# Gated two-layer stack on one core: vector pieces of one link each, layer-1 scores over 32 rows, and the last two transposed blocks of the feed-forward in one operation

## What is computed

```python
x = x + tanh(g_x[0]) * xattn0(layernorm(x), ctx, mask)   # "A": 4 heads of 64, one K/V head, rotary
x = x + tanh(g_f[0]) * ffn0(layernorm(x))                # "F": width 704, inputs in blocks of 16 on an FP4 grid
x = x + tanh(g_x[1]) * xattn1(layernorm(x), ctx)         # "B": 16 heads of 16, biases, no mask
x = x + tanh(g_f[1]) * moe(layernorm(x))                 # "R" routes (top 2 of 8 experts), "M" computes, width 1024
```

```python
Q = (query @ Wq + bq).reshape(B, Tq, 16, 16).transpose(0, 2, 1, 3)
K = (key @ Wk + bk).reshape(B, Tk, 16, 16).transpose(0, 2, 1, 3)
scores = einsum('bhtd,bhsd->bhts', Q, K) / sqrt(16)
ctx = einsum('bhts,bhsd->bhtd', softmax(scores), V)
```

## Time and profile before

| | |
|---|---|
| median of 3 runs | 1644.17 us (1643.66 to 1647.43) |
| profiled execution, its own time | 1642.42 us |
| its span, first to last instruction | 1640.8 us |
| busy over the span: PE, DVE, ACT, POOL | 1400.4, 1117.3, 993.4, 413.3 us |
| mean granted clock of PE | 0.949 |

### The profile page before, as it was taken

How to read it: one execution, slowest core, us unless ns; L and a number is a source line. 1 busy time by engine, 2 the same in 40 slices (tenths; PEclk the granted TensorE clock), 3 DMA queues, 4 the chain that set the end, 5 groups by cost and what they waited for, 6 DMA issues and landing times.

```text
span 1640.8 us, 35711 instructions
## 1 busy us (share of the span) xinstructions
PE 1400.4 (85%) x11645; PEld 1072.6 (65%) x11646; DVE 1117.3 (68%) x2887; ACT 993.4 (61%) x2861; POOL 413.3 (25%) x560
## 2 busy tenths in 40 slices
PE   2567789989999889989998671999999999999994
PEld 1445556665666566656664430888888888888883
DVE  7977779899988999899986534344444454444452
ACT  1244778888888888888876760444445444455542
POOL 0101011211122211212111112334433444344442
PEclk9587999999999999999999975999999999999997
DMA  6020132112320223203220005551231412322214
GB/s 192 13 87 30 62 103 103 45 61 104 103 92 21 95 104 103 72 33 104 94 94 8 8 14 179 177 162 32 33 112 30 114 32 35 108 35 32 35 31 123
DMA packets 63158, 123.58 MB, mean 75 GB/s; under 512 B 13955, under 2 KB 51967, under 8 KB 58879
## 3 DMA queue, kind: packets, MB, share of 16 engines
q1 hardware_dynamic: 45743, 102.75, 18.0%
q0 software_dynamic: 17312, 19.56, 7.2%
HBM read 78.64 MB, written 48.04 MB: 77 GB/s over the span
## 4 chain that ended last, share of the span: by engine, by line
PE 52%; DVE 32%; ACT 8%; issue 5%; DMA 2%; POOL 1%; SPq 0%; DVEq 0%; ACTq 0%; POOLq 0%
PE bank L1401 15%; PE bank L1403 14%; PE bank L1402 14%; DVE b_mn L1121 4%; ACT b_ex L746 3%; PE bank L1483 2%; PE bank L1495 2%; DVE wm L1238 1%; DVE f_hs L1182 1%; DVE split_room L1265 1%; DVE wm L1190 1%; PE bank L1719 1%; DVE x L1176 1%; DVE wm L1196 1%; DVE wm L1201 1%
## 5 line engine op out<-in xcount | busy, mean ns | idle before, releaser
L1401 PE MATMUL bank<-split_room,wm 128*128 128x256 f16 x1152 | 314.9, 273 | 8.2 <-issue 6.8
L1378 DVE SCALAR_TENSOR_TENSOR split_room<-bank,b12e,split_room 128x256 f32<-128x256 f32 x288 | 138.2, 484 | 265.6 <-ACT split_room L900 260.8
L1402 PE MATMUL bank<-split_room,wm 128*128 128x256 f16 x1152 | 314.8, 273 | 0.0
L1403 PE MATMUL bank<-split_room,wm 128*128 128x256 f16 x1152 | 314.7, 273 | 0.0
L900 ACT ACTIVATE split_room<-bank,b12e 128x256 f32<-128x256 f32 x288 | 134.2, 470 | 196.0 <-PE bank L1403 194.2
L746 ACT ACTIVATE b_ex<-bank,b_mn 128x120 f32<-128x120 f32 x512 | 177.0, 361 | 36.9 <-DVE b_mn L1121 28.0
L1403 PE MATMUL bank<-wm,split_room 128*128 128x256 f16 x576 | 157.0, 273 | 0.0
L1401 PE MATMUL bank<-wm,split_room 128*128 128x256 f16 x576 | 157.0, 273 | 0.0
L1402 PE MATMUL bank<-wm,split_room 128*128 128x256 f16 x576 | 157.0, 273 | 0.0
L692 POOL DMA_INDIRECT acc<-split_room,m_cur x72 | 116.1, 1612 | 133.0 <-ACT split_room L914 106.1
L1483 PE MATMUL bank<-b_k,b_q 128*128 128x480 f32 x256 | 131.8, 597 | 14.6 <-ACT b_q L834 14.6
(11 more groups left out here) (356 smaller groups left out, 3616.3 us busy)
## 6 DMA issues: line engine op xcount, KB each, us to landing
split_room<-in_L_ffn_W SPq DMA_DIRECT2D x48, 512.0 KB, 8.0
wsplit<-split_room SPq DMA_DIRECT2D x16, 1536.0 KB, 6.6
wm<-wsplit SPq DMA_DIRECT2D x16, 1536.0 KB, 8.5
acc<-x SPq DMA_DIRECT2D x17, 256.0 KB, 2.2
xin<-in_x SPq DMA_DIRECT2D x16, 256.0 KB
rows<-r_row SPq DMA_DIRECT2D x16, 256.0 KB, 3.7
ct<-in_ctx SPq DMA_DIRECT2D x16, 120.0 KB
cb<-in_ctx SPq DMA_DIRECT2D x16, 120.0 KB, 2.6
```

Of the source, the lines that this page charges most:

```text
L1378: dve.scalar_tensor_tensor(m_h[:, c % 3], bank[c % 4][:, TILE:2 * TILE], b12e[:, p, 1, c:c + 1], m_s[:, c % 2], ALU.add, ALU.mult).then_in ...
L1401: pe.matmul(o, lh, rh, start=start, stop=False)
L1402: pe.matmul(o, ll, rh, start=False, stop=False)
L1403: return pe.matmul(o, lh, rl, start=False, stop=stop)
```

## The change

- Every chain on DVE is cut so that a stage holds one link; the new pieces are named `A.ln_1`, `F.q0a_1`, `R.logit_3` and so on. The operations stay the same.
- B's scores: b_k is now [128, 2, 2, 120]; a group of 32 rows holds two heads, and each of the two copies keeps one of them, so a matmul of 32 rows and 240 columns gives two heads and two of them a round. Head columns of wq1, wk1 and the biases are permuted (`head_order`), b_k is written by two operations over all partitions, and `pair` issues the scores of rounds k and k+1 as four matmuls over 32 rows each, alternating between two row groups and the two banks. The pair waits for the exponentials of all earlier rounds, and DVE's minimum of either round waits for the pair.
- `f_ht_`: blocks 4 and 5 are taken out by one operation on ACT and one on DVE.
- bq arrives by 8 small transfers in place of one, wq1, wk1 and bk are split in portions, and b_k is no longer cleared.
- FIRST, ORDER and LAST are new on all engines. In a steady step DVE's list goes from 57 to 95 entries and PE's from 54 to 50.

The core of the diff:

```diff
-        b_k = sb("b_k", [P, NK, 2, QUAD, S])
+        b_k = sb("b_k", [P, NK, 2, S])
...
-                for j in range(QUAD):
-                    h = slice(PITCH * j, PITCH * (j + 1))
-                    for a in range(2):
-                        last = act.activation(b_k[h, :, a, j], bank[2][h, 0:NK * S].rearrange("p (c s) -> p c s", c=NK), ACT.Copy, scale=C[h, C_M + a:C_M + a + 1])
+                for f in range(2):
+                    last = act.activation(b_k[:, :, f], bank[2][:, 0:NK * S].rearrange("p (c s) -> p c s", c=NK), ACT.Copy, scale=C[:, C_M + f:C_M + f + 1])
...
+                def pair(b, k0):
+                    if k0 == 0:
+                        pe.wait_ge(B.q, b + 1)
+                        pe.wait_ge(B.k, b + 1)
+                    else:
+                        pe.wait_ge(B.exp, b * n + k0)
+                    for e in range(NK):
+                        for k in (k0, k0 + 1):
+                            t, r = k // per, k % per
+                            h = slice(PITCH * r, PITCH * (r + 1))
+                            last = pe.matmul(sbks[k % 2][:, e * 2 * S:(e + 1) * 2 * S], q[h, e, t * P:(t + 1) * P], kk[h, e], start=True, stop=True)
+                            if e == NK - 1:
+                                last.then_inc(B.s_mm, 1)
...
-                        dve.wait_ge(G.s_mm, b * n + k + 1)
+                        dve.wait_ge(G.s_mm, b * n + (k + 1 if G is A else k // 2 * 2 + 2))
...
-                    act.activation(f_ht[:, 0, 4, c], bank[7][:, 0:P], ACT.Copy)
-                    act.activation(f_ht[0:FF0 - 5 * P, 0, 5, c], bank[7][0:FF0 - 5 * P, P:2 * P], ACT.Copy).then_inc(F.hq_hi, 1)
+                    act.activation(f_ht[:, 0, 4:6, c], bank[7][:, 0:2 * P].rearrange("p (c q) -> p c q", c=2), ACT.Copy).then_inc(F.hq_hi, 1)
...
-                    dve.tensor_tensor(f_ht[:, 1, 4, c], bank[7][:, 0:P], f_ht[:, 0, 4, c], ALU.subtract)
-                    dve.tensor_tensor(f_ht[0:r_, 1, 5, c], bank[7][0:r_, P:2 * P], f_ht[0:r_, 0, 5, c], ALU.subtract).then_inc(F.hq_lo, 1)
+                    dve.tensor_tensor(f_ht[:, 1, 4:6, c], bank[7][:, 0:2 * P].rearrange("p (c q) -> p c q", c=2), f_ht[:, 0, 4:6, c],
+                                      ALU.subtract).then_inc(F.hq_lo, 1)
...
+            def f_scale(n):
+                v, m, sc = F_PARTS[n]
+
+                def stage(b, p):
+                    cf.go_on(b)
+                    cf.wait()
+                    cf.link(dve.tensor_scalar(sc[:, 0], sc[:, 2], SIXTH, 1e-12, ALU.mult, ALU.max))
+                return stage
...
+                        for c in range(2):
+                            for a in range(2):
+                                for k in range(NK):
+                                    k_ = slice(k, k + 1)
+                                    split(head_order(st1[:, n_ - 1, k_], c, a, True)[:, 0],
+                                          head_order(w[:, 0, k_], c, a, False)[:, 0], head_order(w[:, 1, k_], c, a, False)[:, 0])
```

More of the change, by code:

```diff
@@ L369, in gated_stack @@
         FIRST = {
[L370 to L371 removed]
[7 rows of a table removed]
[L379 removed]
[11 rows of a table removed]
[L391 removed]
[8 rows of a table removed]
[L400 removed]
+            "SP": ("W@0 A.load@2 B.load@0 B.load@1 A.load@3 W@1 W@2 A.load@4 W@3 B.load@2 B.out@0 B.load@3 R.rank@0").split(),
@@ L444, in gated_stack @@
+            "POOL": ("R.ln@13 R.scatter@13 B.ln@15 R.ln@14 R.scatter@14 R.ln@15 R.scatter@15").split(),
[6 rows of a table added]
+                "B.t6@15 B.t7@15 B.rx1@15 B.r7@15 B.o1@15 R.z@15 R.t@15 R.logit@15").split(),
[11 rows of a table added]
+                "R.rank_4@15 R.rank_5@15 R.rank@15").split(),
[6 rows of a table added]
+                "B.p4@15 B.t5@15 B.t6@15 B.p5@15 B.t7@15 B.p6@15 B.p7@15 B.out@15 R.t@15 R.logit@15 R.rank@15").split(),
         }
@@ L1130, in stage, with values @@
                         ca.link(dve.reciprocal(rd[:, t], pv[:, :, width]))
+                    return stage
+                def values(k):
+                    def stage(b, p):
+                        t = k // per
+                        pv = pbks[t][:, 0:heads * (width + 1)].rearrange("p (h d) -> p h d", h=heads)
+                        ca.go_on(b)
                         ca.wait()
@@ L1137, in rounds @@
                 if G is A:
-                    made.update({f"{G.name}.p{k}": values(k) for k in range(per - 1, n, per)})
+                    made.update({f"{G.name}.p{k}": shares(k) for k in range(per - 1, n, per)})
+                    made.update({f"{G.name}.p{k}_1": values(k) for k in range(per - 1, n, per)})
                 return made
@@ L1205, in f_p @@
-            def f_p(b, p):
-                dequantise(f_z[:, :, :].rearrange("p t d -> p (t d)"), f_m, f_qs[:, 0], b, 0)
-            def f_pt(t):
-                def stage(b, p):
-                    dequantise(f_h[:, t], f_hm[:, t], f_hs[:, t, 0], b, 1 + t)
-                return stage
-            def f_q_in(b, p):
-                cf.go_on(b)
-                dve.wait_ge(F.z, b + 1)
-                for part in (quantise_a, quantise_b):
-                    part(f_z[:, :, :].rearrange("p t d -> p (t d)"), f_m, f_qs, b, 0)
@@ new lines, in f_scale, with stage, f_inverse @@
+            def f_scale(n):
+                v, m, sc = F_PARTS[n]
+                def stage(b, p):
+                    cf.go_on(b)
+                    cf.wait()
+                    cf.link(dve.tensor_scalar(sc[:, 0], sc[:, 2], SIXTH, 1e-12, ALU.mult, ALU.max))
+                return stage
+            def f_inverse(n):
+                v, m, sc = F_PARTS[n]
+                def stage(b, p):
+                    cf.go_on(b)
+                    cf.wait()
+                    dve.reciprocal(sc[:, 1], sc[:, 0]).then_inc(F.v, 1)
+                return stage
@@ new lines, in f_scaled, with stage, f_grid @@
+            def f_scaled(n):
+                v, m, sc = F_PARTS[n]
+                def stage(b, p):
+                    dve.wait_ge(F.v, b * 3 + n + 1)
+                    dve.tensor_tensor(blocks(v), blocks(v), over(sc[:, 1], BLK), ALU.mult).then_inc(F.u, 1)
+                return stage
+            def f_grid(n):
+                v, m, sc = F_PARTS[n]
+                def stage(b, p):
+                    dve.wait_ge(F.abs, b * 3 + n + 1)
+                    dve.tensor_scalar(m, m, 1.5, STEP, ALU.max, ALU.mult).then_inc(F.m, 1)
+                return stage
@@ new lines, in f_round, with stage, f_unshift @@
+            def f_round(n):
+                v, m, sc = F_PARTS[n]
+                def stage(b, p):
+                    dve.wait_ge(F.m, b * 3 + n + 1)
+                    dve.scalar_tensor_tensor(v, v, BELOW, m, ALU.mult, ALU.add).then_inc(F.t, 1)
+                return stage
+            def f_unshift(n):
+                v, m, sc = F_PARTS[n]
+                def stage(b, p):
+                    cf.go_on(b)
+                    dve.wait_ge(F.t, b * 3 + n + 1)
+                    cf.link(dve.tensor_tensor(v, v, m, ALU.subtract))
+                return stage
@@ L1228, in f_q, with f_unscale, stage @@
+            def f_unscale(n):
+                v, m, sc = F_PARTS[n]
+                def stage(b, p):
+                    cf.go_on(b)
+                    cf.wait()
+                    dve.tensor_tensor(blocks(v), blocks(v), over(sc[:, 0], BLK), ALU.mult).then_inc(F.hq, 1)
                 return stage
```

191 lines of the change are left out of this document (112 added, 79 removed), and 129 rows, old and new, of tables (FIRST, LAST, ORDER).

## The result

The changed kernel takes 1674.89 us (median, 1674.34 to 1679.25) against 1644.01 us before: a ratio of 1.019 with an interval of 1.017 to 1.021, so 1.9% slower. The forecast was 1610 us, faster. The profiled execution has a span of 1673.8 us against 1640.8 us.

What follows compares the result with a forecast made beforehand. No engine is full in the 52.2 us step; waits and small gaps on DVE, with PE close, bound it. Twelve steps at 49.2 us give -36 us, lead-in 0, tail +2: span 1606.8, median 1610 us, range 1580 to 1640.

Steps and rivals of the forecast that it cites:

- Part 1: DVE chains cut into pieces: 22 boundaries with other work between, 0.12 us each, 2.6 us less a step (bounds 0 to 5.0).
- One sign: DVE's busy time a step should stay near 47 us, its share rising to about 95%.
- Part 2: Scores over 32 rows on PE: a pair of rounds takes 1.2 us instead of 1.8, 2.4 us of PE less a step.
- Part 3: b_k copies on ACT, two operations instead of eight: 0.7 us instead of 3.21, 2.5 us less a step.
- part 4: f_ht blocks joined: one DVE operation of 0.42 us, saving 0.06 us a call, 0.1 us a step; ACT gains as little.
- part 5: Wait for both rounds: ring 4.9 us, +1.0 us a pair where exposed; in steady steps DVE's work between pairs covers it.
- the sum for the steady step: 52.2 us less 2.6 (pieces), 0.1 (f_ht) and 0.3 (long waits): 49.2 us a step, twelve steps -36 us.
- Part 6: Lead-in before the steady steps taken as 0 (-8 to +8 us); moved loads and POOL entries cost nothing; tail +2 us.
- rival (b): Slower: the wait for both rounds exposes 1.35 us at all four pairs, step 54.6 us, 1679 us in all; chance 0.08.
- The prediction's last sign: The prediction is wrong if the new list brings DVE waits over 3 us a step resting on no old row.
- the size of the end: Tail with two batches of exposed pairs: 7 x 1.0 us more, less 2 x 2.5 us of b_k: +2 us (-4 to +9).
- The start: Lead-in before the steady steps: some 5 us more DVE work against savings in the first batches, taken as 0 (-8 to +8).

Runs made afterwards that it cites:

- a_late2_fill: Changed kernel with R.scatter issued in the next step behind A.t's copies, plus 6 unread matmuls ahead of B.t0 on TensorE: 1623.3 us, 0.989 of the kernel before.
- a_fill: Changed kernel plus 28 unread matmuls a step on TensorE, 12 ahead of B.t0 and 16 behind F.gu0: 1645.4 us, 1.003 of the kernel before.
- b_pairwait: Kernel before with old matmuls and order, scores of both rounds issued together behind all earlier exponentials (TensorE's half of the join only): 1720.3 us, ratio 1.048.
- a_late2_exp: Changed kernel with R.scatter in the next step behind A.t's copies, plus a one-element exponential ahead of R.z on ScalarE: 1641.3 us, 0.999 of the kernel before.
- a_late: Changed kernel with R.scatter's four transfers issued in the next step, behind R.ln on POOL: 1644.3 us, 1.001 of the kernel before.
- a_split: Changed kernel with R.scatter in the next step, two transfers behind R.ln and two behind A.t's copies: 1636.5 us, 0.998 of the kernel before.
- a_late2_rows: Changed kernel, R.scatter in the next step behind A.t's copies, with the old 128-row scores, eight-copy b_k and head order: 1704.0 us, 1.040 of the kernel before.
- a_late2_join: Changed kernel, R.scatter in the next step behind A.t's copies, 21 VectorE pieces put back directly behind the piece they need: 1662.3 us, 1.014 of kernel before.
- a_tail3: a_late2_fill plus 3 unread matmuls ahead of each transposition and pair of scores of the last three batches: 1624.5 us, 0.987 of the kernel before.
- a_tail8: a_late2_fill plus 8 unread matmuls ahead of each transposition and pair of scores of the last three batches: 1632.2 us, 0.992 of the kernel before.

## Why the prediction was wrong, point by point

**Part 1** held in kind: undone, the pieces cost 2.2 us a step, where I had 2.6 (the lists have 14 direct boundaries and 23 others, not 15 and 22). One sign was misread: VectorE's busy time was to stay near 47 us, but of the 0.12 us a pair 0.08 is overlap, which comes off the busy time, and it fell by 1.7 us. **Part 2** was better than taken: 1.01 us a pair and not 1.2, so the 1.80 us of two rounds became 1.8 times as fast. The change of tiling mode, of which the prediction cites a rule from the Trainium skill, is inside that figure: measured against the half of 1.80 us it can be no more than 0.11 us a pair (an estimate), where I had named 0.2. **Part 3** is 0.78 us (0.7 taken) and **part 4** 0.41 us on VectorE (0.42 taken). The new form of a ring of two rounds (**part 5**) is right where nothing else stands in it: the minimum that follows is 4.9 us behind (980.1 to 985.0 us in the tail; 4.9 predicted). The intervals of 6.4, 8.0 and 5.0 us between the first minima of the pairs are 6.6, 8.1 and 5.6 us in a_late2_fill, in the mean of the eleven steps. So the sum for the steady step came out: 49.2 us predicted, 49.5 measured once two things are taken away that it did not hold. That it came out this close is in part luck. Undone in the new order, part 1 costs 2.2 us and parts 2 and 3 cost 4.1, 6.3 us together, where the sum had 2.9 for them; what stands against the surplus, the join and the new order, has no price of its own there.

**What failed first** is a term that was missing. Part 6 said that R.ln's and F.ln's entries on POOL keep their place and cost nothing, and said nothing of R.scatter. It moved, relative to TensorE's work, from A.q1 (400.37 in before) to A.ot. My own row of the 0.92 us wait carried its cost in the kernel before, about 0.4 us of it, and I put all of it down to scores, because the profile names the last semaphore and not why it came late. Held signals and the clock together make the step 54.08 us instead of 49.5: 4.6 us times 11, 50 us.

**What failed second** is the clock, which the prediction took as given since it was 1.00 in all steady steps. With the new TensorE list it falls behind the waits; of the 4.6 us, up to 2.8 go with the clock (a_fill). The mechanism of rival (b), that waits come to all engines at once, had the right size (54.6 us a step, 1679 us in all against 1674.9), but for another reason: the join is exposed in the old order (b_pairwait) and hardly in the new one, whose steps in a_late2_fill are 49.5 us with the join in them, VectorE standing 0.75 us a step for the pairs. The prediction's last sign, new waits of VectorE of more than 3 us a step, was met: in the step from 443.11 us it stands 2.4 us for ScalarE's a_zt and 0.9 for its f_ht, and neither is among the waits of before.

**What failed third** is the size of the end: +2 us taken, bounds -4 and +9, measured +15.4 (10.6 and 4.8). About 6 us of it is the clock. The eight minima of the last batch (tile b_mn in after) span 28.2 us, where before they span 23.6 (951.9 to 975.5):

```profile
L1180 DVE TENSOR_REDUCE b_mn<-bank x8: 647/654/659, 979.5 to 1007.7; 128x4 f32<-128x480 f32 x8
```

That is 4.6 of the 4.8 us. I had read the earlier trace rows as the length of two rounds; it is one round, with the next one in flight beside it. The second pair's ring holds two transpositions and is 8.7 us long (985.6 to 994.3), not 4.9. That the ring makes the 4.8 us is argued from these times; no run shows it.

**The start** was right: 0 taken, -2.8 us measured. The expert loop was unchanged, as said.

## What to carry to other kernels

Read every wait of more than some tenths of a microsecond against all queues, GpSimd's indirect transfers among them: when the producer had ended long before its consumer started, the wait is not that producer's, and a new order can move it to a place where it costs many times as much. When a change makes TensorE's list lighter, ask in which two or three microseconds it now stands, and add to the sum what its clock takes behind them; a few unread matmuls there tell cheaply whether that is so. A join of two rounds costs nothing only where other work fills the queue between, so its price belongs to the order and not to the edit. And look for held signals in the traces of the experiments too, not only in that of the change: three of the kernels here had more of them than the kernels that they were compared with.

## What the runs showed of the hardware

- While four indirect transfers in a row are issued on GpSimd, TensorE's signals can be held for up to 2.6 us in after and 2.8 in a_late2_exp, and land together, in after 0.8 us behind the end of the fourth, in a_late 0.7 us behind it. Without the transfers, and in a_split with the four in two pairs 2 us apart, none was over 0.7 us late; nor in a_late2_fill, a_late2_rows and a_late2_join, with four in a row, while a_tail3 and a_tail8, with the steady lists of a_late2_fill, have them. No signal of VectorE or ScalarE was over 0.7 us late between 250 and 950 us in any of the 17 traces.
- Four f32 matmuls of 32 rows and 240 columns on alternating row groups (eight records): 1.01 us, against 1.80 us for the same columns over 128 rows.
- The granted clock fell from 2.4 to 1.2 GHz for 3.4 us behind 2.07 us of standing, and for 6.8 us behind three microseconds in which TensorE was 0.52, 0.59 and 0.70 busy. 28 added matmuls a step made the kernel 29.5 us faster.
